# Gated attention and routed experts: heads in alternate order with one division, bias and residual by products in PSUM

## The reference

```
q = LN(x) @ Wq + bq;  k, v = ctx @ Wk + bk, ctx @ Wv + bv      (16 heads of 8)
x1 = x + tanh(g_xattn) * (softmax(q k^T / sqrt(8)) v @ W_out + b_out)
gates = softmax(LN(x1) @ Wg);  e = argmax(gates)               (8 experts, 512 slots each)
out = x1 + tanh(g_ffn) * gates[e] * (relu(LN(x1) @ W1[e] + b1[e]) @ W2[e] + b2[e])
```

## Time and profile before

| | us |
|---|---|
| median of three runs | 298.14 |
| the three runs | 301.95, 298.14, 295.5 |
| own time of the profiled execution | 298.6 |
| its span, first to last instruction | 296.5 |

### The profile page before, as it was taken

How to read it: one execution, slowest core, us unless ns; L and a number is a source line. 1 busy time by engine, 2 the same in 40 slices (tenths; PEclk the granted TensorE clock), 3 DMA queues, 4 the chain that set the end, 5 groups by cost and what they waited for, 6 DMA issues and landing times.

```text
span 296.5 us, 8184 instructions
## 1 busy us (share of the span) xinstructions
PE 244.5 (82%) x2907; PEld 163.5 (55%) x2907; DVE 196.6 (66%) x663; ACT 155.6 (52%) x375; POOL 182.3 (61%) x246
## 2 busy tenths in 40 slices
PE   1748758788979989999899989995869999999950
PEld 1325525465755755765656666663324677777740
DVE  4676717647978999989897999965302545555440
ACT  5553727567778787787887756681202322222100
POOL 6625916911982998897897968448720056555781
PEclk9998959969999999999999999999595999999995
DMA  4652771990482652661733541138352256554310
GB/s 120 184 162 73 214 217 32 237 293 19 113 235 57 174 158 71 195 182 46 213 110 90 152 126 57 58 102 174 138 144 66 71 170 188 173 180 132 103 55 16
DMA packets 50920, 39.27 MB, mean 132 GB/s; under 512 B 9698, under 2 KB 47223, under 8 KB 50880
## 3 DMA queue, kind: packets, MB, share of 16 engines
q1 hardware_dynamic: 47168, 28.67, 35.9%
q0 software_dynamic: 3712, 10.07, 10.4%
HBM read 13.72 MB, written 12.65 MB: 89 GB/s over the span
## 4 chain that ended last, share of the span: by engine, by line
PE 39%; DVE 13%; DMA 13%; SPq 10%; issue 9%; ACT 8%; POOL 4%; POOLq 0%; ACTq 0%; DVEq 0%
PE X L634 9%; DMA qp<-mrow 8%; DVE negm L833 6%; SPq L347 6%; PE TS L618 5%; PE M L546 3%; ACT prob L703 3%; PE O L513 3%; PE TS L497 3%; PE O L618 3%; PE M L618 2%; PE S L482 2%; PE X L441 2%; SPq L358 2%; POOL rec_dram L1224 2%
## 5 line engine op out<-in xcount | busy, mean ns | idle before, releaser
L703 ACT ACTIVATE prob<-TS 128x512 f32<-128x512 f32 x128 | 72.0, 589 | 40.1 <-PE TS L497 39.2
L833 DVE TENSOR_REDUCE negm<-S 128x4 f32<-128x512 f32 x128 | 81.6, 679 | 8.5 <-PE S L482 7.9
L513 PE MATMUL O<-prob,vals 128*32 128x128 f32 x1024 | 42.1, 283 | 0.8 <-ACT oraw L712 0.8
L1313 POOL DMA_INDIRECT out_dram<-fin,tok x32 | 31.5, 986 | 14.2 <-issue 12.2
L1224 POOL DMA_INDIRECT rec_dram<-rec,slot x32 | 32.2, 1005 | 8.0 <-issue 5.5
L497 PE MATMUL TS<-qp,kp 64*128 64x128 bf16 x512 | 28.1, 221 | 9.7 <-DMA qp<-mrow 9.6
L482 PE MATMUL S<-kp,qp 62*128 62x128 bf16 x512 | 31.3, 222 | 2.3 <-DVE negm L833 2.0
L513 PEld LDWEIGHTS O<-prob,vals 128*32 128x32 f32 x1024 | 24.6, 110 | 13.9 <-ACT prob L703 7.0
L267 POOL TENSOR_TENSOR rest_k<-full_k,parts_k 128x512 f32<-128x512 f32 x7 | 8.0, 1149 | 39.3 <-ACT parts_k L674 39.3
L804 ACT ACTIVATE qp<-TS,b_act 128x512 f32<-128x512 f32 x16 | 11.0, 687 | 39.9 <-PE TS L618 39.9
L634 PE MATMUL X<-w2s,qp 128*128 128x128 f32 x240 | 28.2, 275 | 0.9 <-issue 0.9
(11 more groups left out here) (170 smaller groups left out, 486.8 us busy)
## 6 DMA issues: line engine op xcount, KB each, us to landing
kp<-parts_k SPq DMA_DIRECT2D x48, 128.0 KB, 2.5
qp<-parts_q SPq DMA_DIRECT2D x48, 128.0 KB, 4.1
rec_dram<-zeros POOLq DMA_DIRECT2D x8, 516.0 KB, 6.2
xr<-rec_dram SPq DMA_DIRECT2D x8, 260.0 KB, 3.9
x_sb<-in_x_dram SPq DMA_DIRECT2D x8, 256.0 KB, 3.6
c_sb<-in_ctx_dram SPq DMA_DIRECT2D x8, 256.0 KB, 3.5
out_dram<-rec SPq DMA_DIRECT2D x8, 256.0 KB, 3.3
w1s<-in_L_ffn_W_dram SPq DMA_DIRECT2D x8, 256.0 KB, 4.1
```

The source lines that it names most:

```text
L513: mm = nc.tensor.matmul(o_out[i * HV:(i + 1) * HV, u * L:(u + 1) * L], vals[G % 2][:, k, h, :], prob[n % 2][:, h * L:(h + 1) * L], start=( ...
L703: nc.scalar.activation(prob[n % 2][:, first:first + 4 * L], TS[:, a, :], ACT.Exp).then_inc(a_exp, 1)
L833: V.tensor_reduce(negm[n % 2][:, first:first + 4], S[:, a, :].rearrange("p (h k) -> p h k", k=L), AX.X, ALU.max, negate=True).then_inc(v_r ...
L1313: G_.indirect_dma_start(out_rows, bass.IndirectOffsetOnAxis(tok[p][:, t:t + 1], 0), fin[p][:, t, :], None, bounds_check=T - 1, oob_is_err= ...
```

## The change

The heads are laid out alternately (even heads in the lower half of the array, odd ones in the upper), so the result comes back in the natural order and one multiplication of 128 columns divides all heads. The product `at` becomes three products into one PSUM bank: first three bf16 parts of the bias (`bout_rows`, 3 rows x 136 columns, with rows of ones as weights), then x_sb with the identity in fp32, then as before onT with W_out. ScalarE copies the 136 finished columns into the record (`rows_kept`); VectorE only takes the statistics, now behind the division. GpSimd's addition for each group goes; once, at step 2, ScalarE and GpSimd split the bias into three parts, which a DMA puts onto three partitions at step 3. Semaphore a_x1 takes the place of v_x1, and waits for it are added in the routing and in norm2. The declarations of semaphores are left out below.

```diff
--- before.py
+++ after.py
@@ -100,6 +100,9 @@
         mean_w = sb("mean_w", [P, P])
+        bout_p = sb("bout_p", [P, 3, DE], BF16)
+        bout_rest = sb("bout_rest", [P, DE])
+        bout_rows = sb("bout_rows", [3, DE], BF16)
         gains = sb("gains", [P, 2])
...
@@ -244,7 +248,7 @@
         emptied = {"v": a_v, "cT": a_cT, "k": a_kf, "xl": v_xl, "pos": v_pos, "xT": a_xT, "q": a_qf,
-                   "m": v_m, "at": v_x1, "back": v_on, "oT": a_oT}
+                   "m": v_m, "at": a_x1, "back": v_on, "oT": a_oT}
 
@@ -298,9 +302,8 @@
                 for a in range(2):
-                    at = i * D + a * HALF
                     sp.dma_start(bqk[a * HALF:(a + 1) * HALF, i:i + 1],
-                                 b_qkv[at:at + HALF].rearrange("(h d o) -> d h o", d=HD, o=1),
+                                 b_qkv[i * D:(i + 1) * D].rearrange("(h a d o) -> a d h o", a=2, d=HD, o=1)[a],
                                  allow_slow_non_contiguous=True).then_inc(s_bias, 16)
@@ -363,7 +366,7 @@
                 if stores:
-                    sp.wait_ge(v_x1, GB * (g - 2) + GB)
+                    sp.wait_ge(a_x1, GB * (g - 2) + GB)
                     sl = bass.ds((g - 2) * GB, GB)
@@ -372,6 +375,10 @@
                     late_loads()
+                if c == 3:
+                    sp.wait_ge(a_bp, 1)
+                    sp.wait_ge(g_bp, 1)
+                    sp.dma_start(bout_rows[:], bout_p[0:1, :, :]).then_inc(s_brows, 16)
                 if j == 1 and 2 <= g + 3 < NG:
@@ -534,8 +541,13 @@
                     bank_free(pe, "at", c - 5)
+                    if c == 5:
+                        pe.wait_ge(s_brows, 16)
+                    pe.wait_ge(v_xl, (c - 5) // GB + 1)
+                    nc.tensor.matmul(X[:, 0, 0:DE], ones_b[0:3, :], bout_rows[:], start=True, stop=False)
+                    nc.tensor.matmul(X[:, 0, 0:DE], ident, x_sb[:, c - 5, :], start=False, stop=False)
                     pe.wait_ge(a_oT, c - 4)
-                    nc.tensor.matmul(X[:, 0, 0:DE], onT[(c - 5) % 2][:], wout_g[:], start=True, stop=True).then_inc(p_at, 1)
+                    nc.tensor.matmul(X[:, 0, 0:DE], onT[(c - 5) % 2][:], wout_g[:], start=False, stop=True).then_inc(p_at, 1)
                 if is_batch(c - 3):
@@ -691,7 +703,7 @@
                     to = vals[G % 2][:, :, a * HH:(a + 1) * HH, a * (HV // 2):a * (HV // 2) + HD]
-                    val = X[:, 1, :].rearrange("p (k h d) -> p k h d", k=GB, d=HD)[:, :, a * HH:(a + 1) * HH, :]
+                    val = X[:, 1, :].rearrange("p (k h a d) -> p k h a d", k=GB, a=2, d=HD)[:, :, :, a, :]
                     mm = nc.scalar.activation(to, val, ACT.Copy)
@@ -701,6 +713,14 @@
                 nc.scalar.activation(prob[n % 2][:, first:first + 4 * L], TS[:, a, :], ACT.Exp).then_inc(a_exp, 1)
+
+            def rows_kept(n):
+                act.wait_ge(p_at, n + 1)
+                G = n // GB
+                if n % GB == 0 and G >= 3:
+                    act.wait_ge(sent[G % 3], zeros_sent(G % 3) + 16 * GB * (G // 3))
+                    act.wait_ge(x1_out[G % 3], 16 * (G // 3))
+                nc.scalar.activation(rec[G % 3][:, n % GB, D:D + DE], X[:, 0, 0:DE], ACT.Copy).then_inc(a_x1, 1)
 
@@ -720,6 +740,8 @@
                     exps(c - 2, 0, 1)
+                if is_batch(c - 5):
+                    rows_kept(c - 5)
                 if j == (2 if g + 2 else 1) and is_group(g + 2):
@@ -758,6 +780,9 @@
                     first_part(0, g + 2)
+                if c == 2:
+                    act.wait_ge(v_wl, 1)
+                    nc.scalar.activation(bout_p[:, 0, :], bout_g[:], ACT.Copy).then_inc(a_bp, 1)
                 if is_batch(c - 4):
@@ -784,6 +809,7 @@
             act.wait_ge(v_nm2, 1)
+            act.wait_ge(a_x1, B)
             normed2((0,))
@@ -838,33 +864,21 @@
 
-            def normalise(n, G):
-                o = back_out.rearrange("p (h a v) -> p a h v", a=2, v=HV // 2)
+            def normalise(n):
+                o = back_out.rearrange("p (h v) -> p h v", v=HV // 2)
                 dve.wait_ge(p_back, n + 1)
                 if n >= 1:
                     dve.wait_ge(v_on, n)
-                V.reciprocal(rl[:].rearrange("p (a h) -> p a h", a=2), o[:, :, :, HD]).then_inc(v_rl, 1)
+                V.reciprocal(rl[:], o[:, :, HD]).then_inc(v_rl, 1)
                 dve.wait_ge(v_rl, n + 1)
                 if n >= 2:
                     dve.wait_ge(p_oT, n - 1)
-                if G is not None:
-                    moments2_ready(G)
-                for a in range(2):
-                    mm = V.tensor_tensor(on[n % 2][:, a * HALF:(a + 1) * HALF].rearrange("p (h d) -> p h d", d=HD),
-                                         o[:, a, :, 0:HD],
-                                         rl[:, a * HH:(a + 1) * HH].unsqueeze(2).broadcast_to([P, HH, HD]), ALU.mult)
-                mm.then_inc(v_on, 1)
+                V.tensor_tensor(on[n % 2][:].rearrange("p (h d) -> p h d", d=HD), o[:, :, 0:HD],
+                                rl[:].unsqueeze(2).broadcast_to([P, HEADS, HD]), ALU.mult).then_inc(v_on, 1)
 
             def residual(n):
-                dve.wait_ge(p_at, n + 1)
-                dve.wait_ge(g_xb, n // GB + 1)
-                G, row1 = n // GB, rec[n // GB % 3][:, n % GB, D:D + DE]
-                if n % GB == 0 and G >= 3:
-                    dve.wait_ge(sent[G % 3], zeros_sent(G % 3) + 16 * GB * (G // 3))
-                    dve.wait_ge(x1_out[G % 3], 16 * (G // 3))
-                V.tensor_tensor(row1, X[:, 0, 0:DE], x_sb[:, n, :], ALU.add).then_inc(v_x1, 1)
-                dve.wait_ge(v_x1, n + 1)
-                V.bn_stats(st2[:, n % GB, :], row1[:, 0:D]).then_inc(v_st2, 1)
+                dve.wait_ge(a_x1, n + 1)
+                V.bn_stats(st2[:, n % GB, :], rec[n // GB % 3][:, n % GB, D:2 * D]).then_inc(v_st2, 1)
 
@@ -910,7 +924,7 @@
                 lgs = rec[G % 3][:, :, 2 * D:2 * D + E]
-                dve.wait_ge(v_x1, GB * G + GB)
+                dve.wait_ge(a_x1, GB * G + GB)
                 if G >= 1:
@@ -1012,9 +1027,9 @@
                 V.tensor_copy(wk_dh[:].rearrange("p (a d h) -> p a d h", a=2, d=HD),
-                              wqkv[:, D:2 * D].rearrange("p (a h d) -> p a d h", a=2, d=HD))
+                              wqkv[:, D:2 * D].rearrange("p (h a d) -> p a d h", a=2, d=HD))
                 V.tensor_copy(wq_dh[:].rearrange("p (a d h) -> p a d h", a=2, d=HD),
-                              wqkv[:, 0:D].rearrange("p (a h d) -> p a d h", a=2, d=HD)).then_inc(s_vset, 1)
+                              wqkv[:, 0:D].rearrange("p (h a d) -> p a d h", a=2, d=HD)).then_inc(s_vset, 1)
 
@@ -1024,10 +1039,12 @@
                     lower_part(c - 1)
+                if is_batch(c - 4):
+                    normalise(c - 4)
                 if is_batch(c - 5):
                     residual(c - 5)
-                if is_batch(c - 4):
-                    normalise(c - 4, g - 2 if j == 0 and is_group(g - 2) else None)
+                if j == 0 and is_group(g - 2):
+                    moments2_ready(g - 2)
                 if j == 0 and is_group(g - 2) and g - 2 < NG - 1:
@@ -1206,6 +1223,7 @@
                 root(G, mv2, rs2, v_mv2, g_e2).then_inc(g_rs2, 1)
+                pool.wait_ge(a_x1, GB * G + GB)
                 scaled(G)
@@ -1244,18 +1262,17 @@
                     G_.tensor_tensor(seen[:], seen[:], mask[:], ALU.add).then_inc(g_seen, 1)
-                if j == 2 and is_group(g):
-                    H = g
-                    pool.wait_ge(a_xn, H + 1)
-                    pool.wait_ge(v_xl, H + 1)
-                    if H == 0:
-                        pool.wait_ge(v_wl, 1)
-                    rows = x_sb[:, H * GB:(H + 1) * GB, :]
-                    G_.tensor_tensor(rows, rows, bout_g[:].unsqueeze(1).broadcast_to([P, GB, DE]), ALU.add).then_inc(g_xb, 1)
+                if c == 2:
+                    pool.wait_ge(a_bp, 1)
+                    G_.tensor_tensor(bout_rest[:], bout_g[:], bout_p[:, 0, :], ALU.subtract).then_inc(g_brest, 1)
+                    pool.wait_ge(g_brest, 1)
+                    G_.tensor_tensor(bout_p[:, 1, :], bout_g[:], bout_p[:, 0, :], ALU.subtract).then_inc(g_brest, 1)
+                    pool.wait_ge(g_brest, 2)
+                    G_.tensor_tensor(bout_p[:, 2, :], bout_rest[:], bout_p[:, 1, :], ALU.subtract).then_inc(g_bp, 1)
                 if j == 3 and is_group(g + 2) and g + 2 != 0:
                     split(pool, G_, 1, g + 2)
                 if j < 3 and is_group(g - 3) and g - 3 < NG - 2:
-                    pool.wait_ge(v_x1, min(c - 4, B))
+                    pool.wait_ge(a_x1, min(c - 4, B))
                     scatter(g - 3, j + 1)
```

5 lines of the change are left out of this document (3 added, 2 removed).

## The result

The changed kernel takes 310.02 us (median of four runs, 306.87 to 311.88), the kernel before beside it 297.81 us (295.5 to 301.95). The ratio is 1.038, 95% interval 1.030 to 1.047: slower. The forecast was 305.5 in a range of 299 to 311; the time lies inside, near its upper end. The increase of 12.2 us was forecast as 6.9 against 298.6, and 7.4 against the median. The direction came out and the mechanism in the main; the size did not.

The account below looks back on a forecast made before the run. The loop was taken to wait for TensorE's transposes back (L546), not VectorE's queue. 298.6 + 5.5 (steps 8 to 24) + 1.4 (steps 25 to 31) = 305.5 us; own range 302 to 308, whole range 299 to 311.

Parts of the forecast that it names:

- some 15 us or more: Total VectorE idle time expected before the reciprocals, about 0.5 us in nearly every step, where 4.5 us stood.
- VectorE's removals gain nothing: Attention loop: removing L865 gains nothing, as it ran in the shadow of L546; one L853 fewer saves 0.07 us.
- The rival with VectorE as the bound: VectorE's queue sets the maxima; steps 8 to 31 each gain 0.37 us, 8.9 in all: 289.7 us; chance 0.12.
- Its own sign: VectorE as the bound holds if L546 comes in the new kernel earlier than 0.4 us behind L839's end.
- TensorE's addition, taken as 0.5 us: Two products ahead of the values and L546 add 0.5 us per step, between 0.3 and 0.67 with both shape changes.
- Steps 8 to 24: 17 loop steps: 1.3 us more per group of four after reserves and the DMA wait, 5.5 us in all.
- Steps 25 to 31: Late loop steps: reserve of up to 0.48 takes nearly all of the 0.5; 0.2 us a step remains, 1.4 us.
- VectorE's 0.13 us: From L546 to the next maxima: statistics leaving the shadow cost 0.20, the single division saves 0.07; net +0.13 us per step.
- Steps 0 to 7 "at nothing": First loop steps hang on DMAs, so the change was charged nothing there.
- nothing there to regain: Removing GpSimd's addition L1254 could shorten VectorE's instructions by the shared-interface rule, but the trace offers no gain; sum unchanged.
- drains in full: Rival: both changes of array shape round the bias product are paid in every step, 0.67 us: 309.2 us; chance 0.15.
- ScalarE's 3 us: Exponentials may come 0.4 us late; charged nothing because a DMA wait covers it, without that cover 8 x 0.4 = 3 us.

Follow-up runs that it names:

- the kernel without products: The changed kernel without the bias product and the x product, so x1 lacks x and the bias; 299.03 us, ratio 0.998 to the kernel before.
- the twin with 128 rows: The kernel before plus one product per batch ahead of L538, 128 rows of ones with zeros, no effect on the output; 299.98 us, ratio 1.011.
- the second attempt at a version that gains: Changed kernel with the bias product over 128 rows, no x product or ScalarE copy, old VectorE order; 313.18 us, ratio 1.013 to the kernel before.

## Why the prediction was right, and where its size was off

*The bound.* Right. The reciprocal starts 0.04 us behind the transposes back in all 32 steps, as it did in 30 of 32 before, and the wait that L865 and L867 had filled appears as idle time. Forecast were "some 15 us or more"; measured are 40.9. Of these 24.7 stand in the kernel without products too and come from the order (7.0 with the old order); the rest is TensorE's longer way. VectorE's share in 100 to 140 us fell to 75% ((13.97 + 16.02) / 40), not to about 85%.

*VectorE's removals gain nothing.* Right. The kernel without products has all of them, and its ratio is 0.998. The rival with VectorE as the bound (289.7) is refuted by the same run and, with VectorE's old order, by the one at 0.993 (0.984 to 1.002). Its own sign is missing as well: in the step shown above the transposes back come 0.51 us behind the lower part's end (188.34 to 188.85), not earlier than 0.4.

*TensorE's addition, taken as 0.5 us.* The term was undersized: it measures 0.59. The x product costs 0.22 (forecast 0.24). The bias product costs 0.11 for itself, twice the 0.05 read off the loads of L466, and 0.25 for its shape. The reading of L466 was wrong in kind: its products have 32 columns in the trace, the bias product 136. The two gaps of 0.17 and 0.20 in the earlier trace rows had made the upper bound 0.37; one of them is paid nearly in full (0.20), the other is 0.05. The Trainium skill (TensorEngine Tiling (Array Packing), section Key Properties) says that changing the tiling mode drains TensorE. The trace agrees in the direction into three rows, with 0.20 us; of a second drain in full it shows nothing.

*Steps 8 to 24.* Forecast 5.5 us for 17 steps, measured 5.9 for 16. The group of four takes 22.6 us in the mean (22.3 from step 16 on) where 22.1 was forecast, and the kernel before has 21.1 in the mean, not 20.8: 1.5 us more, where 1.3 was forecast. The terms come out one by one. TensorE gets 16 x 0.59 = 9.4 us more. The gaps ahead of the transposes back fall from 4.0 to 3.2 us, which gives 0.8 back; the waits for the DMA of the maxima fall from 3.0 us in four cases to 0.5 in one, which gives back 2.5. That leaves 6.1. The table shows in which order the slack went. From no products to 128 rows TensorE gets 16 x 0.34 = 5.4 us more and the stretch grows by 1.7. From there to three rows it gets 4.0 more and the stretch grows by 4.5. The first addition largely fell into reserves and DMA waits; the second met hardly any.

*Steps 25 to 31.* Here a step of the argument failed: "the reserve of up to 0.48 takes nearly all of the 0.5". The 0.68 of the earlier trace rows was one row. The loads of the transposes back in steps 25 to 32 of the kernel before, with the row at 172.65 of the earlier trace rows, show what an average would have been:

```profile
164.16 0.20 PEld L546 LDWEIGHTS M<-cst,oraw 128*128 128x128 f32 x2 [0.20 <-DVE mrow L839]
168.23 0.20 PEld L546 LDWEIGHTS M<-cst,oraw 128*128 128x128 f32 x2 [0.33 <-DVE mrow L839]
...
176.77 0.20 PEld L546 LDWEIGHTS M<-cst,oraw 128*128 128x128 f32 x2 [0.33 <-DVE mrow L839]
182.74 0.20 PEld L546 LDWEIGHTS M<-cst,oraw 128*128 128x128 f32 x2 [0.93 <-DVE mrow L839]
186.81 0.20 PEld L546 LDWEIGHTS M<-cst,oraw 128*128 128x128 f32 x2 [0.33 <-DVE mrow L839]
191.23 0.20 PEld L546 LDWEIGHTS M<-cst,oraw 128*128 128x128 f32 x2 [0.68 <-DVE mrow L839]
194.81 0.20 PEld L546 LDWEIGHTS M<-cst,oraw 128*128 128x128 f32 x2 [0.20 <-DVE mrow L839]
```

Less the 0.20 of the shape, the reserve is 0.13 in three of the eight steps, 0.48 in two, 0.73 in one and nothing in two: 0.26 in the mean. In the changed kernel each of these gaps is 0.20, and the steps without a projection take 4.66 us where 4.07, 4.42 and 4.12 stood. That makes 3.5 us in steps 24 to 32, where 1.4 was forecast for seven steps.

A second term was left out there. The forecast let VectorE's 0.13 us remain in place of TensorE's addition; the trace shows it on top. The second four of the score products wait for VectorE's maxima, and this wait grows; here is the one of step 25, before and after:

```profile
166.53 0.17 PEld L482 LDWEIGHTS S<-kp,qp 62*128 62x128 bf16 x3 [0.19 <-DVE negm L833]
```

```profile
177.38 0.17 PEld L489 LDWEIGHTS S<-kp,qp 62*128 62x128 bf16 x3 [0.32 <-DVE negm L859]
```

Over steps 24 to 32 these waits are 1.4 us before, 2.2 in the changed kernel, 2.2 in the kernel without products and 1.0 in that kernel with the old order on VectorE, so it is the order that makes them. The sum is 8 x 0.59 = 4.7, less 2.1 of gaps ahead of the transposes back (3.7 to 1.6), plus 0.8: 3.4 us, against 3.5 measured.

*Steps 0 to 7 "at nothing".* This failed too in the profile. The changed kernel is 1.5 us later at step 4 and loses 2.6 more to step 8. The 1.5 us can't be the products', since the first of them stands in step 5, nor the splitting of the bias in steps 2 and 3, which the kernels without products (49.32) and with 128 rows (48.40) have too. The granted clock between 24 and 50 us is 0.63 in its profile and 0.80 in that of the kernel before (the earlier trace rows begin later), and over the profiles of this document the start of step 4 goes with it: 45.65 us at 0.93, 48.40 and 48.48 at 0.87, 49.13 to 49.78 at 0.80, 49.28 and 49.81 at 0.67, 50.41 and 50.74 at 0.64 and 0.63. The stretch from 4 to 8 doesn't follow the clock. It takes 24.93 to 28.83 us over all profiles: 27.18 in the kernel without products, 28.83 in the second profile of the changed kernel, 25.54 in the one with the x product alone. Its cause is open.

*ScalarE.* Right: the copy adds work (8.8 us) and no time that the kernel without products would show.

*GpSimd: "nothing there to regain".* As said of L1254 this stands: in the trace of the kernel before no VectorE instruction was lengthened beside it. Contention of VectorE with other GpSimd instructions does stand there, as the last section shows. The forecast's sum isn't touched: the kernel without products, which lacks the addition, stays at 0.998.

Summed for the changed kernel by timed ratios: order, division, ScalarE and the removals 0.998, the x product and the bias product in 128 rows up to 1.023 (+2.5%, 7.5 us), the shape up to 1.038 (+1.5%, 4.6 us). The rival "drains in full" (309.2) came near in time but not in its mechanism: of the second gap it counted 0.05 us stands there, and the missing part came from the early and late steps. That the time still lies in the range of 299 to 311 is partly luck: the range's upper end was set by gaps paid in full and by a part of ScalarE's 3 us, and neither happened. The forecast gave the loop 6.9 us and the profiles show 13.5. Of the 6.6 us that it was short, 4.1 stand in steps 0 to 8, 0.4 in steps 8 to 24 and 2.1 in steps 24 to 32.

## What to carry to other kernels

In this loop, work moved onto TensorE was free only where TensorE idled at that very place; read the gap ahead of its next dependent load in every step of a group, and take the mean of all rows, not the largest. A product with few contraction rows between full ones costs more than its columns (here 0.36 us a step against 0.11): fill the rows with zeros, or put it next to a product after which the shape changes anyway. An instruction removed from the shadow of a wait gains nothing. One pushed out of that shadow costs up to its distance (0.13 us a step for the statistics, 0.53 for sum and statistics in the late steps), less where other waits absorb it.

## What the runs showed of the hardware that was not expected

*A VectorE instruction of four elements was held until GpSimd's addition ended.* In the kernel with the product of three rows added, in the timeline of step 26:

```profile
169.99 2.08 DVE L952 SCALAR_TENSOR_TENSOR over<-loc,none_c 128x4 f32<-128x4 f32 x1
...
170.69 1.36 POOL L1259 TENSOR_TENSOR x_sb<-x_sb,bout_g 128x544 f32<-128x544 f32 x1
...
172.00 0.15 DVE L953 SCALAR_TENSOR_TENSOR base<-choice,loc 128x4 f32<-128x4 f32 x1
...
173.53 0.27 DVE L843 TENSOR_TENSOR mrow<-M,mrow 16x128 bf16<-16x128 f32 x1
...
173.85 0.29 PEld L550 LDWEIGHTS M<-cst,oraw 128*128 128x128 f32 x2 [2.30 <-DVE mrow L843]
```

L952 takes 0.16 us in the kernels and steps where it is not held. Here it takes 2.08 and ends 0.03 us behind GpSimd's L1259 (172.05). It began 0.70 us ahead of L1259, while GpSimd finished an indirect DMA issue (L1229, to 170.47) and a small addition (L1251, 170.49 to 170.75); what held it before L1259 isn't shown. The maxima behind it are late, and TensorE idles 2.30 us before the transposes back. Then its granted clock goes from the 2.4 GHz level to the 1.2 GHz level:

```profile
165.00:170.00 5.00, 4.79 (x83) 3.10 (x82) 4.70 (x15) 3.64 (x12) 4.74 (x5) 1.00 0.48 136
170.00:175.00 5.00, 2.97 (x46) 1.95 (x44) 4.55 (x10) 1.23 (x4) 4.23 (x6) 0.77 0.46 138
175.00:180.00 5.00, 5.00 (x63) 3.09 (x59) 3.62 (x9) 2.86 (x7) 0.00 (x0) 0.50 0.09 31
180.00:185.00 5.00, 5.00 (x49) 3.68 (x47) 3.30 (x15) 1.08 (x2) 2.00 (x5) 0.50 0.19 57
```

Steps 24 to 32 take 44.92 us there instead of 37.11 in the twin with 128 rows, in which the same instruction takes 0.16. The kernel with the bias on GpSimd (1.94 us, TensorE idle 2.27) and the one with only the order changed (1.18 us, idle 1.76) show the same in the same step, and there too the instruction ends 0.03 us behind the addition. In the kernel before, and in the twin, the instruction begins 1.3 to 1.4 us ahead of the addition and takes 0.16. So it seems to hang on where the addition falls. That the hold makes the stall, and the stall the loss of several microseconds, is read from the order of events; the one attempt to move the addition away got rid of the hold and not of the stall, as told below. The Trainium skill (GPSIMD Engine Reference, section Specifications) says that the SBUF interfaces are shared with VectorE, with contention for instructions with two SBUF inputs. The trace agrees in how these holds end; the 0.70 us by which one began too early it leaves open. In the kernel before, the group of this instruction and the one in the changed kernel:

```profile
L948 DVE SCALAR_TENSOR_TENSOR over<-loc,none_c 128x4 f32<-128x4 f32 x7 | 2.9, 411 | 0.2
```

```profile
L962 DVE SCALAR_TENSOR_TENSOR over<-loc,none_c 128x4 f32<-128x4 f32 x7 | 1.1, 163 | 0.2
```

So the effect was in the trace of before already (411 ns in the mean, at the most 1.10 us at 129.73, ending 0.02 us behind GpSimd's L270), where no one waited for it. There the partner is the splitting of q into parts (L268, L270), not the addition of the bias. In the changed kernel the splits are still there and no longer meet it; in the second attempt at a version that gains, without GpSimd's addition, it still takes 1.05 and 1.14 us in two of the groups.

*A stall of 2 us late in the loop without this cause.* On the third chip TensorE stands still for about 2 us and its clock falls around step 26 in the changed kernel too, which has no such addition:

```profile
185.98 0.09 PEld L539 LDWEIGHTS M<-cst,negm 128*16 128x16 f32 x1 [2.13 <-issue]
```

The granted clock is 0.59 from 185 to 190 us. In the version with GpSimd's addition one step later L944 takes 0.16 us in that step, and TensorE still idles 1.95 us before L545. In both ScalarE stands as well: 2.64 us before its copy L791 in the one, 1.97 us before the exponential L702 in the other, from which the rows of maxima, L838 and L545 follow. The releaser of these two waits lies outside what the profile records ("remote"), so the cause stays open. All four profiles on that chip have the stall around step 26, so it may also have part in the stalls blamed on the hold above. Whether the transposes back could be freed of their wait for L839 by a bank of their own was not tried.
